# The second sorted expert layer's border: roots of its second half between the first half's sends, its route ahead of the first tile, sends from tile 0 on

## The reference, cut to what matters

```
x = x + _L2_xattn_ref(_layernorm(x), ctx_768, ...)
x = x + _L2_ffn_ref(_layernorm(x), ...)

def _L2_ffn_ref(x, ln_g, ln_b, rW, rb, W1, b1, W2, b2):
    z = _layernorm(x, ln_g, ln_b)
    logits = jnp.einsum('bth,he->bte', z, rW) + rb
    probs = jax.nn.softmax(logits, axis=-1)
    topv, topi = jax.lax.top_k(probs, TOP_K)
    ...
    hid = jax.nn.gelu(jnp.einsum('bth,ehf->btef', z, W1) + b1, approximate=False)
    outs = jnp.einsum('btef,efh->bteh', hid, W2) + b2
    return x + jnp.sum(outs * w[..., None], axis=2)
```

## Time and profile before

| | |
|---|---|
| median of 3 runs | 748.54 us (744.16 to 759.54) |
| the profiled execution | 746.98 us |
| its span, first to last instruction | 744.3 us |
| mean granted TensorE clock | 0.931 |
| PE, DVE, ACT, POOL busy in the span | 609.6, 490.0, 405.5, 335.8 us |
| att2's last projection on PE ends | 504.78 us after the span's start |
| the 46 sorted tiles of moe2 on PE | 518.5 to some 585 us |

### The profile page before, as it was taken

One profiled execution on the slowest core, in us unless ns is written; L12 is line 12 of the kernel. 1 busy time (PEld: TensorE's weight loads), 2 busy tenths in 40 slices (PEclk: granted clock), 3 DMA queues, 4 the chain that ended last, 5 costly groups with the idle time before them and its releaser, 6 DMA issues. The chain is left out here.

```text
span 744.3 us, 15830 instructions
## 1 busy us (share of the span) xinstructions
PE 609.6 (82%) x4682; PEld 431.8 (58%) x4682; DVE 490.0 (66%) x1477; ACT 405.5 (54%) x944; POOL 335.8 (45%) x491
## 2 busy tenths in 40 slices
PE   2677889899998987799987777864899867879996
PEld 1355565444443433799964455543788666746864
DVE  4677766788789753555767877552766657674665
ACT  4366556477776665366643465452677644544521
POOL 4445455344333146071746765155436573154035
PEclk9999999989999999699985999795799989999999
DMA  6254443222222101043435353101244410022544
GB/s 174 75 132 113 110 106 81 71 75 77 72 76 74 53 24 43 29 136 106 130 90 145 104 133 82 30 33 47 89 140 141 159 44 4 3 96 82 146 120 120
DMA packets 93010, 66.29 MB, mean 89 GB/s; under 512 B 11024, under 2 KB 85392, under 8 KB 92704
## 3 DMA queue, kind: packets, MB, share of 16 engines
q1 hardware_dynamic: 87808, 54.79, 26.8%
q0 software_dynamic: 5120, 10.50, 4.6%
HBM read 29.11 MB, written 16.88 MB: 62 GB/s over the span
## 5 line engine op out<-in xcount | busy, mean ns | idle before, releaser
L1116 DVE TENSOR_REDUCE negmax<-ps 128x2 f32<-128x512 f32 x256 | 170.1, 686 | 79.2 <-PE ps L2427 77.5
L2016 ACT ACTIVATE exps<-ps 128x512 f32<-128x512 f32 x256 | 150.2, 600 | 81.4 <-PE ps L2440 79.6
L2427 PE MATMUL ps<-stack 96*128 96x256 bf16 (+1 forms) x512 | 103.8, 299 | 23.0 <-DVE negmax L1116 21.0
L2440 PE MATMUL ps<-stack 99*128 99x256 bf16 (+1 forms) x512 | 100.0, 285 | 18.1 <-DMA stack<-maxt 11.8
L1815 POOL DMA_INDIRECT gathered<-z,placed x64 | 62.3, 974 | 53.6 <-PE ps L2803 28.1
L1833 POOL DMA_INDIRECT late<-outputs_moe,placed x64 | 62.2, 972 | 47.4 <-PE ps L2803 25.1
L2440 PEld LDWEIGHTS ps<-stack 99*128 99x128 bf16 (+1 forms) x512 | 37.4, 99 | 76.9 <-issue 39.5
L2478 PE MATMUL ps<-exps,values 128*32 128x256 f32 x1024 | 77.7, 397 | 0.3 <-issue 0.3
L2427 PEld LDWEIGHTS ps<-stack 96*128 96x128 bf16 (+1 forms) x512 | 39.5, 102 | 44.8 <-DVE negmax L1116 35.0
L2819 PE MATMUL ps<-pack_moe,ht 128*128 x368 | 59.6, 286 | 1.7 <-DVE y_kept L1538 0.6
L2819 PEld LDWEIGHTS ps<-pack_moe,ht 128*128 128x128 f32 x368 | 49.2, 195 | 4.8 <-issue 3.4
(11 more groups left out here) (232 smaller groups left out, 1379.4 us busy)
## 6 DMA issues: line engine op xcount, KB each, us to landing
stack<-qk_parts SPq DMA_DIRECT2D x96, 128.0 KB, 2.5
outputs_moe<-y_kept SPq DMA_DIRECT2D x115, 64.0 KB
stack<-qk_parts SPq DMA_DIRECT2D x96, 64.0 KB
ht<-gathered SPq DMA_DIRECT2D x44, 128.0 KB, 2.4
stack<-weights_t SPq DMA_DIRECT2D x16, 256.0 KB, 3.5
pack_moe<-in_moe SPq DMA_DIRECT2D x11, 256.5 KB, 3.2
pack_moe<-in_moe SPq DMA_DIRECT2D x6, 429.5 KB
gathered<-y_kept SPq DMA_DIRECT2D x10, 256.0 KB, 2.8
```

Of the source, the lines that this page charges most:

```text
L1116: dve.tensor_reduce(negmax_of[b % 2][:, :, h:h + 1].rearrange("p t h -> p (t h)"), ps[:, h % 2, :].rearrange("p (t k) -> p t k", t=2), AX, ...
L2016: nc.scalar.activation(exps[:, i, :], ps[:, 2 + h % 2, :], ACT.Exp, scale=scale)\
L2427: return pe.matmul(ps[:, h % 2, t * T:(t + 1) * T], st[:, 0, t * P:(t + 1) * P], st[:, 1, :], start=True, stop=True)
L2440: return pe.matmul(ps[:, 2 + h % 2, t * T:(t + 1) * T], st[:, 1, t * P:(t + 1) * P], st[:, 0, :], start=True, stop=True)
```

## The change

It does five things, all for moe2 alone; moe1 keeps its order.

- The statistics of group 3 move from after the tail to beat (3, 4), directly behind the residual of batch 7, ahead of the z of group 2 (L1062), which stays at (3, 5).
- The roots of group 2 move from (2, 5) to (2, 0), and those of group 3 from after the sends to (2, 3). For these two groups only row 0 is made there; row 1, for token tiles 8 to 15 at once, is made after the last send (`make_late_roots`), and `keep_of_norm` waits for it.
- xb for att2's batches 6 and 7 is made by DVE right behind the residual of the batch before (`BIAS_AFTER`), and no longer by POOL at beat 3.
- The whole route of the second half (logits, picks, marks, ranks, place) stands ahead of the tile loop on PE and DVE. Only the expert index stays at step 3.
- `SEND_TILE` is 0 for moe2: send n waits for tile 9n/10.

```
-    "moe2": {"stats": ((-2, 5), (-1, 5), (2, 5)), "rstd": ((-2, 7), (-1, 7), (2, 5)),
+    "moe2": {"stats": ((-2, 5), (-1, 5), (2, 5), (3, 4)), "rstd": ((-2, 7), (-1, 7), (2, 0), (2, 3)),
...
-SEND_TILE = 4
+SEND_TILE = {"moe1": 4, "moe2": 0}
+BIAS_AFTER = {("att2", B - 3): B - 2, ("att2", B - 2): B - 1}
...
             def keep_of_norm(s):
+                wait(dve, "rstd_ready", s, 0, len(NORMED[s]))
...
             def residual(s, d):
...
+                if (s, d) in BIAS_AFTER:
+                    b = BIAS_AFTER[s, d]
+                    wait(dve, "x_updated", s, d)
+                    bo = par(s, "bo").unsqueeze(1).to_broadcast([P, 2, D])
+                    dve.tensor_tensor(xb[:, :, :], x_sb[:, 2 * b:2 * b + 2, :], bo, ALU.add).then_inc(sem["xb_ready"], 1)
...
             def sorted_tiles(s):
                 down_bias = load_down_bias(s, 0) if s == "moe2" else None
+                if s == "moe2":
+                    route_logits(s, 1)
+                    pick_by_logit(s, 1)
+                    mark_picks(s, 1)
+                    place_tokens(s, 1, 0)
+                    place_tokens(s, 1, 1)
                 for j in range(-2, ALL_TILES + 2):
...
             def experts(s):
-                    stats_all(s, len(NORMED[s]) - 1, NORMED[s][-1])
+                    stats_all(s, len(NORMED[s]) - 1, NORMED[s][-1]) if s == "moe1" else None
...
-                if s == "moe2":
+                if s == "moe2" and g < 2:
                     last = pool.tensor_scalar(var_eps[:, 1, ts], moments[:, ts, 1], 1.0, EPS, ALU.mult, ALU.add)
...
+            def make_late_roots():
+                s, g, ts = "moe2", len(NORMED["moe2"]), slice(NORMED["moe2"][2][0], NT)
+                pool.tensor_scalar(var_eps[:, 1, ts], moments[:, ts, 1], 1.0, EPS, ALU.mult, ALU.add).then_inc(sem["var_ready"], 1)
+                wait(pool, "var_ready", s, 0, g)
+                pool.tensor_tensor(rstd[:, 1, ts], var_eps[:, 1, ts], neghalf[:, 1, ts], ALU.pow).then_inc(sem["rstd_ready"], 1)
...
-                        if u == BIAS_BEAT[heads] and valid(d) and sd != "att0":
+                        if u == BIAS_BEAT[heads] and valid(d) and sd != "att0" and (sd, d - 1) not in BIAS_AFTER:
                             add_bias(sd, d)
...
-                    wait(pool, "taken_psum", s, 0, SEND_TILE + n * 9 // 10)
+                    wait(pool, "taken_psum", s, 0, SEND_TILE[s] + n * 9 // 10)
...
-                make_rstd_all(s, len(NORMED[s]) - 1, NORMED[s][-1])
+                make_rstd_all(s, len(NORMED[s]) - 1, NORMED[s][-1]) if s == "moe1" else make_late_roots()
...
                 turn_all(s, [len(CHUNKS[s]) - 1])
+                if s == "moe2":
+                    logits(s, 1, NORMED[s][-1])
+                    rank_tokens(s, 1)
                 for j in range(-2, ALL_TILES + 2):
...
-                    if j == SORT_BEATS[s]["logits"]:
+                    if s == "moe1" and j == SORT_BEATS[s]["logits"]:
```

21 lines of the change are left out of this document (10 added, 11 removed).

## The result

The changed kernel takes 742.7 us (median of 20 runs, 735.35 to 753.79), the kernel before 748.64 (20 runs beside it). The ratio is 0.9915 with a 95% interval of 0.989 to 0.994: 6.4 us less, between 4.5 and 8.2. That is inside 2%, and the predicted time was 744.5 in a range of 738 to 752.

What follows compares the result with a forecast made beforehand. PE bounds the tiles at 1.14 us each, so time before the first and stalls between them move the end one for one; 2.0 us in front plus 2.0 at tile 23 takes 748.54 to 744.5 us, range 738 to 752.

Steps and rivals of the forecast that it cites:

- The sum: Whole change: 2.0 us at the first tiles plus 2.0 at tile 23, 4.0 us less, 744.5 us; chance 0.56.
- clock stays: Rival, PE before the first tiles: high clock holds, total gain some 8 us, or 6.5 for half (742.0); chance 0.12.
- Roots and last send: POOL, first half's sends: with roots made in parts the last send starts at 512.8, against 512.93 before.
- Statistics and z: DVE behind att2's last projection: z of group 2 starts at 506.3, 5.2 us earlier, and lg at 515.1.
- The route in front: DVE, lg to `placed`: 6.05 us, `placed` 6.2 us earlier; the price is that the first `gated` stands behind it.
- The clock: PE, first tiles: logits stay at the low clock, the rise comes at 526.8, 2.7 us earlier; 1.6 taken as 2.0.
- a first load by SP after 517: Sign of being wrong, SP's queue: its loads behind the first half's sends, forecast at 515.3, would start later than 517.
- The middle: PE at tile 23: earlier sends remove the stall, 2.2 us of tile 22 to 26's 6.72, of which 2.0 taken.
- Only the middle: Rival, front: lg comes at 516.7, tile 4 does not move, only the stall's 2.0 us remain, 746.5; chance 0.14.
- The stall stays: Rival, tile 23: the last send lands after 547, SP waits as before, only the front wins, 746.5; chance 0.09.
- The slower rival: Route in front, lg not earlier: 3.6 us lost at tile 4, 2.0 won at tile 23, 1.6 slower, 750.1; chance 0.09.

Runs made afterwards that it cites:

- r_before: The kernel before, unchanged, profiled a second time; no ratio given; it waited 3.08 us at tile 23 and took 9.72 us from tile 22 to 26.
- e5: The changed kernel with the bias additions of att2's batches 6 and 7 back on GpSimd; 751.78 us, ratio 0.9935 to the kernel before.
- e4: The kernel before with only the route in front and the sends from tile 0 on added; 745.84 us, ratio 0.9954 to the kernel before.
- e3: The changed kernel with the second half's route back beside the first tiles; 745.54 us, ratio 0.9943 to the kernel before.
- e10: The changed kernel with tile 0 transposed ahead of the ranks; 740.12 us, ratio 0.985 to the kernel before; run again 743.82 us, 0.9942.
- e8: The changed kernel with unread filler products on TensorE between the projection and tile 1; 747.21 us, ratio 1.0011 to the kernel before.
- e1: The changed kernel with the second half's sends from tile 4 on again; 746.37 us, ratio 0.9954 to the kernel before.
- e6: The changed kernel with the second half's sends only from tile 8 on; 758.05 us, ratio 1.0111 to the kernel before.
- e9: The changed kernel with the route beside the tiles and sends from tile 4 on, leaving the front alone; 744.68 us, ratio 0.9998 to the kernel before.
- e2: The kernel before with only moe2's sends changed, to start from tile 0 on; 748.11 us, ratio 0.9989 to the kernel before.
- r_e2: A second profile of e2's kernel, the first being of a disturbed execution; no ratio of its own; it waited 2.66 us at tile 23.

## Why the prediction was right

**The sum.** Predicted were 2.0 us in front and 2.0 in the middle. From A the first pair of profiles gives 1.96 to tile 4, 0.10 from there to tile 22 and 2.12 to tile 26: the steps came out nearly as written, and the forecast of 744.5 misses by 1.8 us. Against r_before it is 0.78, -0.27 and 5.12 instead, so how near the steps came depends on which execution of the kernel before is taken. Two pieces of luck belong here. The range of 738 to 752 held every case of the prediction, so the time alone could hardly speak against it. And 742.7 lies nearer to the 742.0 of the rival "clock stays" than to the forecast: that the forecast's mechanism was at work is shown by the profiles and not by the median.

**Roots and last send.** "The last of four more sends starts at 509.0 + 3 x 1.26 = 512.8", which is A + 8.0: measured A + 7.79. The added xb was priced at 0.42 from VectorE's x_sb; it took 0.43.

**Statistics and z.** z "5.2 us earlier": it moved from A + 6.68 to A + 1.18, 5.5. In r_before z was at A + 5.49, so the gain there is 4.3: before, z hangs on GpSimd's queue and not on A, so the distance shrinks when the last projection is late by itself. e5 shows that the bias on VectorE carries 2.1 of it in that execution.

**The route in front.** 6.05 us from lg to `placed`: 6.17. Its price at tile 4 was right as well (from z 3.54 us more, in e4 3.66), and e3 adds what the prediction did not separate: 1.2 us of it is the step itself, and e10 gets back 1.5 by one turned step, since tile 0's rows were there 2.5 us before TensorE took them.

**The clock.** It fell before the new z, at 506.7, and came back at 530.6, 6.1 us after tile 1's transpose (524.53) where 5.1 was taken from the dense start: the rival "clock stays" fell. The rise, at A + 22.6, is behind tile 4 (A + 21.04), so the 0.4 us that the prediction gave to the clock up to there was not the clock's: lg came 0.4 us earlier than foreseen (A + 9.90 against 10.3). From tile 4 to tile 8 it took 5.80 us against 5.97. One sign of being wrong came true by its letter, "a first load by SP after 517": it was at 518.15, but that is A + 10.15, where before it was at A + 10.55. e8 forced the clock to stay; lg came 1.5 us earlier by it, as the rival had it (1.4), tiles 4 to 8 won 0.7 us, and the fillers in the queue took 1.0 ahead of tile 4. What a clock kept without cost would be worth was not tried. The Trainium skill ("TensorE: Matmul & The Clock Gate", "What's actually happening") ties the clock to TensorE's activity; e8's windows agree (0.83 to 1.00 with fillers, 0.50 without).

**The middle.** "So the stall goes: 6.72 - 4 x 1.14 = 2.2 us, of which I take 2.0". The mechanism is confirmed from both sides (e1, e6: sends later, wait back; e3, e9: tiles earlier and sends later, wait back). SP's load of tile 23 came at A + 38.9 where the prediction has A + 37.5: it carries tiles 23 and 24 (128 KB) and waits for tile 18, not 17, and its rows, 2.0 us later, were still 3.5 us ahead of tile 23. **The size is the term that was off**: it was priced from one execution with a wait of 1.46 us. Over eight profiles with a wait, two prices show. Waits of 1.45 to 2.21 us cost themselves and 0.7 to 1.0; waits of 2.66 us and more cost themselves and 1.9 to 2.1, because the clock is then at 0.50 behind tile 23 and two or three tiles run at 1.2 GHz. The windows bear this out in all eight: the granted clock stays at 1.00 behind tile 23 in before, e3 and e9 and stands at 0.50 two us behind the start of tile 23's transpose in r_before, e1, e2, r_e2 and e6. So the 0.7 to 1.0 of the short waits is not the clock's price; in e9 the next tile came 1.90 us behind tile 23, with 0.30 us of it spent waiting for DVE's `gated`. The kernel before had 6.72 us in one profile and 9.72 in the other, so the middle is worth 2.1 or 5.1 us. With the front of the same profile (2.0 or 0.8 us at tile 4), the layer's end moves by 4.2 us against the first and 5.1 against the second, and 5.1 is within the measured 4.5 to 8.2, where 4.0 was just outside. The rest up to 6.4 lies in no stretch that the profiles single out, and stays open.

**The rivals.** "Only the middle" fell with tile 4 at A + 21.04. "The stall stays" fell here but is what e1, e2 and e9 show. The slower rival decides from an lg 4 us late; e4 built that case, and it was faster than before: its loss of 3.6 in front was right, its 2.0 in the middle too small.

**Neither half alone.** Sends from tile 0 alone showed no gain (0.9989, 2.9 us faster to 1.3 slower), the front alone none either (0.9998, 2.7 faster to 2.4 slower), the whole change 6.4 us. Of the kernels that lack one part of the change, e1, e3, e4 and e5 are each faster than the kernel before, and their intervals overlap the changed kernel's, so how the 6.4 us divide is read from the profiles and not from the ratios. The front pulls the tiles towards the last landing and so lengthens the wait; the sends alone are held by `placed`, which the front makes early. The prediction added two terms that showed their sum only together.

## What to carry to other kernels

Where a stream of tiles runs into a landing, price the stall from several executions and by what it does to the clock: a wait here cost up to 1 us beyond itself where the clock stayed at 1.00 (waits of 1.45 to 2.21 us) and about 2 us where it fell to 0.50 (2.66 to 7.23 us). Two edits, one that moves the consumer earlier and one that moves the producer earlier, are to be priced as a pair, by the slack between them; here the schedule had to leave 4.5 to 6.5 us from the last send's start to the tile, the more where a packet of the `instruction` queue fell between, so look into the DMA records before calling a long landing scatter. Compare stages by their distance from an event that the change cannot move, since this border lay between 500.07 and 516.23 us in the fourteen profiles, and 11 us apart in two of the same kernel (e2 at a mean clock of 0.915, r_e2 at 0.933).
